# Attention outputs brought to head order by DMA transposes of scaled f16 parts, with a reordered prologue

## Chip, cores and metric

The kernel runs on one core of one Trainium2 chip. The metric is the device time of one execution in microseconds (us); less is better. All weights and the hidden states start in device memory and the result is written back there.

## What is computed

One transformer layer on `h` of 2 x 1024 tokens x 256 channels, 16 heads of width 128, one shared key and value head:

```python
q = rmsnorm(rope(h @ Wq_c @ Wq_up)) * q_norm_w           # 16 heads x 128
k = rmsnorm(rope(h @ Wk)) * k_norm_w;  v = h @ Wv
ck = rmsnorm(h.reshape(b, 64, 16*256) @ W_comp)          # one compressed key per block of 16 tokens
c_out  = softmax([q @ ck.T * s  (earlier blocks only), sink]) @ ck
sw_out = softmax([50*tanh(q @ k.T * s / 50)  (last 64 tokens), sink]) @ v
ao = c_out + sw_out
x = layernorm(h + (ao grouped by 4 heads @ Wg).reshape(...) @ Wo)
y = layernorm(x + x @ ternary(ffn_weight).T + bias)
```

The kernel folds `Wg` and `Wo` into one matrix per head, `Weff` (128 x 256), and multiplies the compressed values with it once (`CW`), so that the compressed half of the attention goes straight from probabilities to the 256 output channels.

## The kernel before

**Tiles and steps.** The 2048 tokens are 16 tiles of 128. One loop (`all_steps`) is written out in full, once for each engine, for steps i = -1 to 17. In step i the engines work on four tiles at once: the queries of tile i+1 (`front`), the attention of tile i (`mid`), the output projection and first norm of tile i-1 (`proj`), and the feed forward part and second norm of tile i-2 (`ffn`). A tile looks at `n = groups(i)` = i mod 8 + 1 groups of 8 compressed keys, so the compressed scores, their exponentials, the transposes of their probabilities and the products with `CW` grow with n.

**Order.** There is no planner. Each engine (TensorE = PE, VectorE = DVE, ScalarE = ACT, GpSimd = POOL, SyncE = SP) has its instructions in a fixed order, written by hand, and waits on counting semaphores. So an instruction that waits holds back all that stands behind it on its engine.

**One step on PE**: queries of the next tile (line 443, banks 0 to 3), transposes of `x1` (519), 12 window score matmuls (546) with the feed forward matmuls (526) between them, compressed scores (560), 36 matmuls of the projection of the tile before (600, heads 0 to 11, `EARLY`), the product of the probabilities with `V` for the first 64 queries (621, `values(0)`), the remaining 12 projection matmuls, the products with `CW` (579), `values(1)`, the transposes of the compressed probabilities (639, `probs_T`), and 16 transposes of the attention output `ao` into PSUM (648, `output_T`). Only then the next step's queries.

**Three products for one.** Where f32 accuracy is wanted, an operand is split in a high part and the rest (`PARTS`: high x high, low x high, high x low). The projection takes `ao` and `Weff` in f32r parts: ACT writes the high part of the transposed `ao` from PSUM (`narrow`, line 672), DVE the rest (`output_rest`, line 1027).

**DVE in a step**: sums of squares of the queries (945), the second norm's sum `z` (953, it waits for `g_out`, the result of the tile before, since `z` has one buffer), rope of half the queries (963, 964), the maximum of the compressed scores (974), the rest of rope, the norm (993), `divide(0)` (1009 to 1020), `query_rest` (1035), the first norm's sum (1045), `divide(1)`, then `output_rest` twice.

**ACT in a step**: two squares of queries (731), the copy of the transposed `x1`, four tanh (745), two exp (749), 16 exponentials of compressed scores (758), the f16 part of the queries (line 672 by way of `narrow`, which writes `room_K`), the copy of the transposed probabilities, and the two high parts of `aoT`.

**POOL in a step**: a power for the query norm (1112), two masks (1106), the normalisation of the compressed probabilities (1120), a power (1126), `x1` (1130), `x1` plus bias (1134), and the result (1137, `g_out`).

**SP in a step**: four DMA transposes of the queries (350), f16, 128 partitions x 1024 elements each, which PE's window scores wait for (`s_qt`), and the output (365).

**Prologue.** Loads, transposes of `h`, keys and values, compressed keys, then `xcT` (the latent queries), the transposes of `Wg`, the key norm and rope, the ternary weights, `Weff` (484 and 721, rest on DVE 934), `CW` (506), which goes through device memory (`cw_rows`) to be laid out by block. In step -1 ACT writes all eight high parts of `Weff` (`output_weights`) and then the two f16 parts of tile 0's queries.

## Time and profile before

| | |
|---|---|
| median of 3 runs | 455.08 us (454.64 to 455.99) |
| profiled execution, its own time | 455.08 us |
| its span, first to last instruction | 453.1 us, so 2.0 us lie around it |
| PE busy | 407.7 us (90%) |
| DVE busy | 351.8 us (78%) |
| ACT busy | 277.0 us (61%) |
| POOL busy | 227.7 us (50%) |
| granted TensorE clock, mean | 0.97 of full speed |

Matmuls overlap on PE, so the duration of one (some 280 ns) is longer than the distance to the next; the chain of work gives the length of a whole group. A wait is listed in brackets with what ended it. The first window scores start at 77.4 us; from there to 406.9 us the loop runs 15 times, and the last stretch to 453.1 us has no queries of a next tile.

### The profile page before, as it was taken

What the parts mean: (1) busy time and instruction counts of PE and PEld (TensorE: products, weight loads), DVE (VectorE), ACT (ScalarE), POOL (GpSimd) and SP (SyncE); (2) the same over time, 40 slices, a digit from 0 to 9 for tenths busy, and PEclk for the clock granted to TensorE, in tenths of its full rate; (3) what the DMA queues carried; (4) which work ended last, traced back from release to release, by engine and by line L of the source; (5) the groups of instructions that cost most, each with busy time, mean ns of one, the idle gap of its engine ahead of it and who ended that gap; (6) DMA issues with size and microseconds to landing.
All of it is one profiled execution on the core that took longest, in us unless ns stands there. A gap on an engine that the chain in (4) does not pass through costs nothing.

```text
span 453.1 us, 9004 instructions
## 1 busy us (share of the span) xinstructions
PE 407.7 (90%) x3361; PEld 350.7 (77%) x3363; DVE 351.8 (78%) x668; ACT 277.0 (61%) x802; POOL 227.7 (50%) x151
## 2 busy tenths in 40 slices
PE   6997888599898999999999999898989999998991
PEld 5996777479696878787879797787788888887880
DVE  3557897788898988889788878888798898972422
ACT  3556527857667675858484848584859595847200
POOL 2743120606456565656564636565546565654505
PEclk9999699889999999999999999999899999999997
DMA  8990007292242406040605060406050604060000
GB/s 257 259 341 9 1 0 210 94 255 53 44 59 48 93 14 94 14 93 13 95 13 93 13 92 16 93 13 95 12 94 13 94 14 93 14 94 13 0 13 23
DMA packets 80651, 33.43 MB, mean 74 GB/s; under 512 B 68960, under 2 KB 79200, under 8 KB 80352
## 3 DMA queue, kind: packets, MB, share of 16 engines
q1 hardware_dynamic: 79792, 32.53, 33.4%
q8 instruction: 27, 0.44, 0.4%
q10 hardware_dynamic: 816, 0.33, 0.3%
q14 instruction: 16, 0.13, 0.1%
HBM read 11.87 MB, written 4.19 MB: 35 GB/s over the span
## 4 chain that ended last, share of the span: by engine, by line
PE 59%; DVE 16%; issue 9%; ACT 9%; POOL 3%; DMA 2%; SPq 1%; POOLq 0%; ACTq 0%; DVEq 0%
PE PS L600 12%; PE PS L546 9%; PE PS L621 9%; PE PS L443 5%; ACT room_h L758 5%; PE PS L560 4%; DVE room_wg L1020 4%; PE PS L579 4%; PE PS L648 3%; PE PS L526 3%; PE PS L405 3%; DVE room_K L1035 2%; DVE aoT L1027 2%; PE PS L484 2%; PE PS L422 2%
## 5 line engine op out<-in xcount | busy, mean ns | idle before, releaser
L600 PE MATMUL PS<-Weff,aoT 128*128 128x256 f32 x768 | 97.1, 282 | 0.0
L600 PEld LDWEIGHTS PS<-Weff,aoT 128*128 128x128 f32 x768 | 91.6, 188 | 0.1
L1112 POOL TENSOR_TENSOR ny<-nx,nu 128x16 f32<-128x16 f32 x16 | 46.7, 2920 | 89.0 <-DVE nx L947 89.0
L1106 POOL TENSOR_TENSOR room_wg<-room_comp,keep 128x1024 f32<-128x1024 f32 x32 | 75.9, 2394 | 6.2 <-ACT room_comp L749 6.2
L621 PE MATMUL PS<-V,room_wg 128*128 128x129 f32 x512 | 67.8, 283 | 6.9 <-POOL room_wg L1106 2.5
L621 PEld LDWEIGHTS PS<-V,room_wg 128*128 128x128 f32 x512 | 63.4, 196 | 11.1 <-ACT room_h L758 4.0
L758 ACT ACTIVATE room_h<-PS,room_K 128x8 f32<-128x8 f32 (+7 forms) x256 | 70.4, 363 | 1.8 <-DVE room_K L974 1.7
L758 ACT ACTIVATION_READ_ACCUMULATOR room_h<-PS,room_K 128x1 f32 x256 | 62.0, 248 | 0.0
L672 ACT ACTIVATE room_wo<-PS 128x128 f32<-128x128 f32 (+7 forms) x16 | 10.4, 651 | 75.1 <-PE PS L639 75.1
L1027 DVE TENSOR_TENSOR aoT<-PS,aoT 128x1024 fp32r<-128x1024 f32 x32 | 38.9, 1224 | 16.8 <-ACT aoT L672 16.5
L546 PE MATMUL PS<-room_h,kT 128*128 128x512 f16 x192 | 46.5, 379 | 2.5 <-DVE aoT L1027 1.3
L648 PE MATMUL PS<-ident,room_wg 128*128 128x128 f32 x256 | 35.2, 282 | 14.6 <-DVE room_wg L1020 14.2
L1126 POOL TENSOR_TENSOR ny<-nx,nu 128x2 f32<-128x2 f32 (+1 forms) x17 | 11.6, 682 | 70.0 <-DVE nx L1054 70.0
L745 ACT ACTIVATE room_comp<-PS 128x512 f32<-128x512 f32 x64 | 36.7, 604 | 15.8 <-PE PS L546 15.6
L672 ACT ACTIVATE aoT<-PS 128x1024 fp32r<-128x1024 f32 x32 | 32.8, 1024 | 21.1 <-PE PS L648 20.9
L648 PEld LDWEIGHTS PS<-ident,room_wg 128*128 128x128 f32 x256 | 28.9, 144 | 19.2 <-DVE room_wg L1020 18.4
L1020 DVE TENSOR_TENSOR room_wg<-PS,r 128x768 f32<-128x768 f32 x64 | 41.3, 686 | 1.1
L945 DVE TENSOR_REDUCE ssq<-room_wg 128x8 f32<-128x1024 f32 x32 | 37.7, 1211 | 3.0 <-ACT room_wg L731 2.8
L443 PE MATMUL PS<-wqup_p,xcT 128*128 128x512 f32 x128 | 36.2, 420 | 2.6 <-DVE xcT L874 1.5
L1035 DVE TENSOR_TENSOR room_K<-PS,room_K 128x1024 f16<-128x1024 f32 x32 | 37.7, 1219 | 0.5
L993 DVE TENSOR_TENSOR PS<-PS,ny 128x1024 f32<-128x1024 f32 x32 | 37.7, 1223 | 0.0
L1120 POOL TENSOR_TENSOR room_h<-room_h,room_K 128x112 f32<-128x112 f32 (+7 forms) x16 | 22.2, 1386 | 26.5 <-DVE room_K L1013 26.5
(151 smaller groups left out, 744.6 us busy)
## 6 DMA issues: line engine op xcount, KB each, us to landing
H<-in_L_attn_h SPq DMA_DIRECT2D x4, 512.0 KB, 6.3
room_wg<-in_L_attn_Wg SPq DMA_DIRECT2D x1, 2048.0 KB, 15.3
cw_rows<-room_wgT SPq DMA_DIRECT2D x1, 2048.0 KB, 6.8
CW<-cw_rows SPq DMA_DIRECT2D x1, 2048.0 KB, 8.1
out<-room_wo SPq DMA_DIRECT2D x16, 128.0 KB, 1.7
CW<-in_L_attn_Wq_up SPq DMA_DIRECT2D x2, 512.0 KB, 12.3
room_wo<-in_L_attn_Wo SPq DMA_DIRECT2D x1, 1024.0 KB, 17.7
room_h<-room_K SPq DMA_TRANSPOSE x64, 3.3
```

The costliest lines, as they stand in the source:

```text
L443: last = nc.tensor.matmul(qbank(hf)[:, (n % 2) * 512:(n % 2 + 1) * 512], xcT[:, t * P:(t + 1) * P], wqup_p[:, w, n * 512:(n + 1) * 512], s ...
L546: last = nc.tensor.matmul(bank(b), kT[:, kp, at + c * WIN:at + c * WIN + P], qT[:, qp, 8 * hf:8 * hf + 8, c * WIN:(c + 1) * WIN], start=n ...
L600: last = nc.tensor.matmul(o, aoT[:, ap, hd // 2, hd % 2, :, :].rearrange("p c q -> p (c q)"), Weff[:, wp, hd, :], start=mid and hd == n == ...
L621: last = nc.tensor.matmul(pv, Pm[:, c, 2 * pr:2 * pr + 2, :], V[:, 2 * i + c, :], start=True, stop=True)
L648: last = nc.tensor.transpose(bank((2, 4)[c], 2)[:, pr * P:(pr + 1) * P], ao[:, c, pr, :], ident[:, :])
L672: nc.scalar.activation(dst, src, ACT.Copy).then_inc(s, 1)
L758: last = nc.scalar.activation(Ec[:, 0:n, hd], bank(4 + hd // 8)[:, (hd % 8) * n:(hd % 8 + 1) * n], ACT.Exp, bias=mn[:, hd:hd + 1], accum_o ...
L1020: last = V_.tensor_tensor(o, pv, r, ALU.mult)
L1027: V_.tensor_tensor(aoT[:, 1, :, :, c, :], bank((2, 4)[c], 2).rearrange("p (a r q) -> p a r q", r=2, q=WIN), aoT[:, 0, :, :, c, :].bitcast( ...
L1035: V_.tensor_tensor(qp[:, 1, heads, :], by_head(hf), qp[:, 0, heads, :], ALU.subtract).then_inc(d_ql, 1)
L1106: G.tensor_tensor(Pm[:, c, :, :], E[:, c, :, :], keep[:, :, :], ALU.mult).then_inc(g_mask, 1)
L1112: G.tensor_tensor(ny[:, 0:HEADS], nx[:, 0:HEADS], nu[:, 0:HEADS], ALU.pow).then_inc(g_rs, 1)
```

## The change

- The 16 PE transposes of `ao`, ACT's and DVE's splits of them from PSUM, and the semaphores p_at and d_al go. Instead ACT writes `ao` in f16 from SBUF to SBUF (`output_high`, one for each half c of the tile), POOL writes the rest in f16 (`output_low`; the first behind line 1120, the second behind line 1134 and ahead of line 1137), and SP issues four DMA transposes for each tile (`outputs`), each of 64 partitions x 2048 elements of f16.
- `Weff`, `ckTv` and `aoT` are f16. So that f16 holds them, the values and `Weff` are scaled by powers of two, worked out in the prologue from sums of squares (`total`, `norms`, `unit`); DVE takes the scale out again in the first norm's sum.
- The projection is 32 matmuls with the high part (`project_high`), then, behind `values(0)`, 16 with the low part (`project_low`).
- The transposed probabilities use banks 2 and 3, not 0 and 1.
- On ACT the first square of the next-but-one tile's queries stands between the copy of the transposed probabilities and `output_high(1)`.
- Prologue: other order of loads (`Wq_up` behind `Wg`), of PE's groups (queries of tile 0 and key transposes ahead of the transposes of `Wg`), key rope before the key norm, the ternary weights on POOL, eight sums of squares on ACT, tile 0's f16 queries written between the high parts of `Weff`, some fifteen small chained instructions on DVE for the scales, the rests of `Weff` (`weights_rest`) spread over more places in step -1, a room of its own for `staged`, and the read of `CW` issued ahead of tile 1's query transposes.

```diff
@@ sync: new, behind queries(i + 1) in each step
+            def outputs(i):
+                wait(sp, p_o, i)
+                for n, ready in ((0, a_at), (1, g_al)):
+                    sp.wait_ge(ready, 2 * i + 2)
+                    for r in range(2):
+                        sp.dma_start(aoT[:, n, r, :, :].rearrange("p a (c q) -> p (a c) q", q=WIN),
+                                     ao16[r * WIN:(r + 1) * WIN, n, :, :, :].rearrange("p a c d -> p (a c d)"),
+                                     transpose=True).then_inc(s_ah if n == 0 else s_al, 16)
@@ tensor: step
-                    wait(pe, *((d_al, 2 * t - 3) if hf else (a_ct, t - 1)))
+                    wait(pe, d_ql, 2 * t + hf - 1)
+                    if hf:
+                        wait(pe, a_ct, t - 1)
...
-                    pe.wait_ge(a_at, 2 * t + 2)
-                    pe.wait_ge(d_al, 2 * t + 2)
...
+                    pe.wait_ge(s_ah, 32 * t + 32)
+                def project_high():
+                    for hd in range(HEADS):
+                        for wp in range(2):
+                            last = nc.tensor.matmul(o, aoT[:, 0, hd % 2, hd // 2, :], Weff[:, wp, hd, :],
+                                                    start=mid and hd == wp == 0, stop=False)
+                def project_low():
+                    pe.wait_ge(s_al, 32 * t + 32)
+                    for hd in range(HEADS):
+                        last = nc.tensor.matmul(o, aoT[:, 1, hd % 2, hd // 2, :], Weff[:, 0, hd, :],
+                                                start=False, stop=not mid and hd == HEADS - 1)
...
-                def output_T(c):
-                    pe.wait_ge(d_ao, 2 * i + c + 1)
-                    for pr in range(PAIRS):
-                        last = nc.tensor.transpose(bank((2, 4)[c], 2)[:, pr * P:(pr + 1) * P], ao[:, c, pr, :], ident[:, :])
-                    last.then_inc(p_at, 1)
@@ scalar: step
-                    def output_T(c):
-                        act.wait_ge(p_at, 2 * i + c + 1)
-                        narrow(aoT[:, 0, :, :, c, :], bank((2, 4)[c], 2).rearrange("p (a r q) -> p a r q", r=2, q=WIN), a_at)
+                    def output_high(c):
+                        act.wait_ge(d_ao, 2 * i + c + 1)
+                        wait(act, s_ah, 32 * i)
+                        narrow(ao16[:, 0, :, c, :], ao[:, c, :, :], a_at)
+                    output_high(0)
                     act.wait_ge(p_ct, i + 1)
...
+                    if i + 2 < NT:
+                        square(i + 2, 0)
+                    output_high(1)
@@ vector: step
-                    wait(dve, p_at, 2 * i + c - 1)
+                    wait(dve, g_al, 2 * i + c - 1)
...
-                def output_rest(c):
-                    dve.wait_ge(a_at, 2 * i + c + 1)
-                    V_.tensor_tensor(aoT[:, 1, :, :, c, :], bank((2, 4)[c], 2).rearrange("p (a r q) -> p a r q", r=2, q=WIN),
-                                     aoT[:, 0, :, :, c, :].bitcast(f32), ALU.subtract).then_inc(d_al, 1)
@@ gpsimd: step
+                def output_low(c):
+                    pool.wait_ge(a_at, 2 * i + c + 1)
+                    wait(pool, s_al, 32 * i)
+                    G.tensor_tensor(ao16[:, 1, :, c, :], ao[:, c, :, :], ao16[:, 0, :, c, :], ALU.subtract).then_inc(g_al, 1)
@@ scalar: prologue
+                    nc.scalar.mul(Weff[:, 0, 2 * g:2 * g + 2, :], two(G_WE + g), w_unit).then_inc(s_wh, 1)
+                    if g in (4, 5):
+                        act.wait_ge(s_ps, G_CKT + 1)
+                        query_high(0, g - 4)
@@ vector: prologue
+            dve.wait_ge(s_ps, G_SC + 1)
+            V_.tensor_copy(total[:, :], gbank(G_SC)[:, 0:8]).then_inc(s_evd, 1)
+...
+            link(V_.reciprocal(unit[:, 0:2], unit[:, 2:4]))
+            V_.tensor_tensor(o_inv[:, :], v_inv, w_inv, ALU.mult).then_inc(s_unit, 1)
@@ gpsimd: prologue
+            G.tensor_scalar(fw_a[:, :, :], fw_s[:, :, :], fthr[:, 0:1], fscale[:, 0:1], ALU.is_gt, ALU.mult)
+            pool.wait_ge(s_fth, 2)
+            G.tensor_scalar(fw_b[:, :, :], fw_s[:, :, :], fthn[:, 0:1], fscale[:, 0:1], ALU.is_lt, ALU.mult).then_inc(s_fth, 1)
+            pool.wait_ge(s_fth, 3)
+            G.tensor_tensor(wfT[:, :, :], fw_a[:, :, :], fw_b[:, :, :], ALU.subtract).then_inc(s_fw, 1)
```

## Rows read from the trace of the kernel before

**Rows 1.** Stages: length, busy us of PE, PEld, DVE, ACT, POOL, PE clock, DMA share
```profile
77.00:98.60 21.60, 16.02 (x124) 12.54 (x125) 16.59 (x30) 14.18 (x46) 7.94 (x4) 0.84 0.60 176
...
162.00:183.70 21.70, 20.79 (x187) 17.93 (x185) 19.38 (x37) 15.17 (x47) 13.01 (x8) 1.00 0.36 57
...
229.20:253.40 24.20, 23.15 (x195) 19.67 (x194) 20.14 (x37) 15.91 (x47) 13.83 (x8) 1.00 0.28 50
...
297.50:320.50 23.00, 21.12 (x180) 17.98 (x179) 20.29 (x38) 15.03 (x47) 12.47 (x8) 0.93 0.35 59
...
406.90:453.10 46.20, 33.44 (x259) 28.73 (x260) 14.51 (x34) 13.71 (x45) 17.24 (x14) 0.93 0.04 12
```

**Rows 2.** Chain of work: start, length, what; last row from a later step
```profile
164.35 1.29 PE PS L546 x6
...
167.11 4.18 PE PS L600 x36
...
172.64 0.73 PE PS L621 x4
...
180.60 1.09 PE PS L648 x8
181.69 1.83 PE PS L443 x8
...
245.99 1.79 PE PS L621 x16
```

**Rows 3.** DVE in the step from 162.1 us, idle time before in brackets
```profile
164.69 0.42 DVE L953 TENSOR_TENSOR room_wo<-PS,room_h 128x256 f32<-128x256 f32 x1
...
175.21 2.36 DVE L1035 TENSOR_TENSOR room_K<-PS,room_K 128x1024 f16<-128x1024 f32 x2
...
179.25 1.29 DVE L1020 TENSOR_TENSOR room_wg<-PS,r 128x768 f32<-128x768 f32 x2
180.86 1.22 DVE L1027 TENSOR_TENSOR aoT<-PS,aoT 128x1024 fp32r<-128x1024 f32 x1 [0.32 <-ACT aoT L672]
```

**Rows 4.** ACT in that step: first exponential, then the f16 parts of the queries
```profile
168.07 0.32 ACT L758 ACTIVATE room_h<-PS,room_K 128x40 f32<-128x40 f32 x1
...
172.38 2.02 ACT L672 ACTIVATE room_K<-PS 128x1024 f16<-128x1024 f32 x2
```

**Rows 5.** POOL in that step: the result
```profile
181.75 1.22 POOL L1137 TENSOR_SCALAR room_wo<-room_wo,mv,ny 128x256 f32<-128x256 f32 x1
```

**Rows 6.** POOL in the prologue
```profile
41.24 1.17 POOL L1086 TENSOR_TENSOR room_comp<-room_K,rope_s 128x256 f32<-128x256 f32 x1 [10.23 <-DVE room_K L876]
...
43.52 0.73 POOL L1086 TENSOR_TENSOR room_comp<-room_K,rope_s 128x256 f32<-128x256 f32 x1
...
47.73 1.90 POOL L1092 TENSOR_TENSOR keep<-CW,e 128x1024 f32<-128x1024 f32 x1 [2.81 <-ACT e1w L709]
```

**Rows 7.** Groups by line: shapes, xcount, busy us, mean ns, idle time before
```profile
L1106 POOL TENSOR_TENSOR room_wg<-room_comp,keep 128x1024 f32<-128x1024 f32 x32 | 75.9, 2394 | 6.2 <-ACT room_comp L749 6.2
...
L579 PE MATMUL PS<-CW,room_wo 128*128 128x256 f32 (+1 forms) x144 | 33.7, 379 | 0.0
```

**Rows 8.** DMA transposes of line 350: ns of SP to issue, us to landing
```profile
L350 SPq DMA_TRANSPOSE room_h<-room_K x64: 1231/1327/2367, 69.7 to 402.3; - x64
...
DMA to landing us min/median/max: 3.2/3.3/5.1
```

**Rows 9.** Chain of work from the weights to the first window scores
```profile
56.47 2.36 DVE ssq L945 x2
...
68.63 1.94 ACT room_K L672 x2
...
73.93 3.34 DMA room_h<-room_K
77.40 2.77 PE PS L546 x12
```

**Rows 10.** Last tile: transposes of its attention output on PE
```profile
427.67 2.27 PE L648 MATMUL PS<-ident,room_wg 128*128 128x128 f32 x16
```

More of the change, by code:

```diff
@@ L382, in _ @@
             pe.wait_ge(s_id, 2)
-            for n in range(12):
+            for n in range(14):
                 nc.tensor.transpose(bank(7)[:, 0:P], ident[:, :], ident[:, :])
@@ L445, in queries @@
                     last.then_inc(p_q, 1)
-            for g in range(G_WG - 8, G_WG):
-                if g % 8 < 4:
-                    copied(pe, g)
-            pe.wait_ge(s_up, 1)
-            pe.wait_ge(s_lo, 4)
-            queries(0)
+            pe.wait_ge(s_up, 2)
+            pe.wait_ge(s_lo, 1)
+            for g in (9, 10, 11, G_CK):
+                copied(pe, g)
+            queries(0)
+            pe.wait_ge(s_kn, 1)
+            for g in range(4):
+                b = begin(G_KT + g)
+                for t in range(4):
+                    last = nc.tensor.transpose(b[:, t * P:(t + 1) * P], K[:, 4 * g + t, :], ident[:, :])
+                end(last)
+            pe.wait_ge(s_kn, 2)
+            b = begin(G_CKT)
+            end(nc.tensor.transpose(b[:, 0:P], K[:, NT, :], ident[:, :]))
             pe.wait_ge(s_wg, 16)
@@ L461, in _ @@
                 end(last)
-            pe.wait_ge(s_kn, 1)
-            for g in range(4):
-                b = begin(G_KT + g)
-                for t in range(4):
-                    last = nc.tensor.transpose(b[:, t * P:(t + 1) * P], K[:, 4 * g + t, :], ident[:, :])
-                end(last)
-            b = begin(G_CKT)
-            end(nc.tensor.transpose(b[:, 0:P], K[:, NT, :], ident[:, :]))
+            pe.wait_ge(s_tot, 8)
+            b = begin(G_SC)
+            end(nc.tensor.matmul(b[:, 0:8], ones[:, :], total[:, :], start=True, stop=True))
             pe.wait_ge(s_fs, 1)
@@ L693, in _, with squares, latent @@
             nc.scalar.activation(sqk, K[:, 0:NT, :], ACT.Square).then_inc(s_sq, 1)
-            if by_scalar[G_CK]:
-                evac(G_CK, K[:, NT, :], gbank(G_CK)[:, 0:D])
-            for g in range(4):
+            def squares(n, data):
+                wait(act, s_tot, n)
+                nc.scalar.activation(junk.rearrange("p (a d) -> p a d", d=data.shape[2]), data, ACT.Square,
+                                     accum_out=total[:, n:n + 1]).then_inc(s_tot, 1)
+            def latent(g):
                 act.wait_ge(s_ps, G_XC + g + 1)
@@ L723, in step @@
             def step(i, front, mid, proj, ffn):
-                if front:
-                    for hf in range(2):
-                        act.wait_ge(p_q, 2 * i + 3 + hf)
-                        if i == -1:
-                            act.wait_ge(s_ps, G_WG + 8)
-                        wait(act, d_red, 2 * i + 2)
-                        wait(act, p_pv, 2 * i)
-                        nc.scalar.activation(sq[:, 8 * hf:8 * hf + 8, :],
-                                             qbank(hf).rearrange("p (a d) -> p a d", d=D),
-                                             ACT.Square).then_inc(a_sq, 1)
+                if front and i < 1:
+                    square(i + 1, 0)
@@ L978, in step @@
                 if first:
[L979 removed]
+                    weights_rest(1)
                 if front:
@@ L987, in step @@
                         last.then_inc(d_add, 1)
+                if first:
+                    weights_rest(2)
                 if front:
```

304 lines of the change are left out of this document (174 added, 130 removed).

## The prediction

> **What bounds the kernel now.** I read the stages first [rows 1]. From 77.4 to 406.9 us the loop makes 15 rounds, 329.5 us in all. The step from 162 us (n = 5) is typical: 21.7 us, PE busy 20.8, DVE 19.4, ACT 15.2, POOL 13.0. PE leads, but DVE is only 1.4 us behind it, so I followed the chain of work next. In this step it leaves PE after the product with `V` (172.64), runs through DVE's `divide(0)`, `query_rest`, the first norm's sum and `divide(1)` (ends at 180.54), and comes back with the second batch of transposes of `ao` at 180.60, for which PE had stood idle about 0.9 us; then queries, then window scores at 183.7 [rows 2, 3]. So two things hold the step: PE's own queue, and the way over DVE and back. At n = 8 the step is 24.2 us with PE busy 23.2: there it is PE's queue alone [rows 1]. Two stages ran at less than full clock (0.84 in the first, 0.93 from 297.5) [rows 1]. Then I read each engine's own list in the one step, to see who gets slack and who gets work.
>
> **PE, what goes.** 16 transposes: two batches of 1.09 = 2.2 us at most (the first partly overlaps what is ahead), and the 0.9 us idle between them [rows 2]: about 2.9 us at n = 5, 2.0 where PE didn't wait. The projection stays 48 matmuls of 256 columns. Now 36 take 4.18, 116 ns each [rows 2]. An f16 one of 512 columns takes 1.29 / 6 = 215 ns [rows 2], so 256 columns take 107 if columns set the pace and 116 if nothing is gained; I take 110, a gain of 0.3 us a step, bounds 0 to 0.4. By its own queue PE would need 21.7 - 2.9 - 0.3 = 18.5 us at n = 5. It won't get there, because of what follows.
>
> **DVE** loses two operations of 1.22 us [rows 3]: 2.4 us off 19.4, so 17.0. The scale in the first norm's sum adds an operand that is one number for each partition: nothing, at most 0.1.
>
> **ACT** writes the same number of elements, from SBUF and not from PSUM. The nearest row is its f16 part of the queries, 2.02 / 2 = 1.01 us for 1024 elements [rows 4]; I take 1.0, bounds 0.8 to 1.2. No work is added, but the order changes: `output_high(1)` now stands behind `probs_T`'s copy and the square of the next-but-one tile, and this square waits for the first half of its queries on PE.
>
> **POOL** gets two `output_low` of 1024 elements a step. No row has this operation with f16. The masks, same size and two inputs, take 2.39 us [rows 7]; one operation of that size with broadcast inputs took 1.90 [rows 6]; and the rope product took 1.17 us for 256 elements while DVE was also at work, 0.73 after DVE had stopped [rows 6], that is 4.7 us for 1024 at the worst. I take the mask's 2.4, since it runs in the same loop beside the same DVE, bounds 1.9 to 4.7. POOL goes from 13.0 to 17.8 us: not full. But the second one stands **ahead of the result (1137)**, and DVE's `z` (953) waits for the result of the tile before, having one buffer. Before, the result ended at 182.97 and the next `z` came some 3.3 us later [rows 3, 5], so nobody saw this wait. 2.4 us more, plus the later start behind `output_high(1)`, eat it up.
>
> On this the Trainium skill (GPSIMD Engine Reference, specifications) says that POOL shares its SBUF interfaces with DVE and that they contend with DVE instructions that have two SBUF inputs. The two rope rows agree. In the loop DVE's large operations read PSUM, so by that rule the slow price doesn't apply.
>
> **The new round (R).** It closes over four engines. At n = 5, from rows: `z` to the first exponential 168.07 - 164.69 = 3.4, less about 0.4 in which DVE waited for the scores = 3.0; 16 exponentials 172.38 - 168.07 = 4.3 [rows 3, 4]; the last quarter of the product with `V` 0.7 [rows 2]; 16 low matmuls at 110 ns 1.8; products with `CW` of the tile before, 4 groups at 33.7 / 72 = 0.47, less the slow stages = 1.8 [rows 7]; `values(1)` 1.8 [rows 2]; 5 transposes of probabilities (0.5) and half the queries (0.9) with the way to ACT, 1.7 [rows 2]; the square 1.0; `output_high(1)` 1.0 [rows 4]; `output_low(1)` 2.4; the result 1.2 and two hand-overs 0.1 [rows 5]. Sum **20.8 us**. Per further group it grows by about 0.9 (exponentials and maximum 0.3, `CW` 0.45, transposes 0.1 and so on): 21.7, 22.6, 23.5 for n = 6, 7, 8.
>
> **The short round (S)**, for small n, goes by DVE alone: `z` 164.69 to the end of `divide(1)` 180.54 is 15.9, less the 0.4 = 15.5 [rows 3]; then `output_high(1)`, `output_low(1)` and the result, 4.7: 20.2 at n = 5, 0.13 less per group: 19.7 to 20.0 for n = 1 to 4.
>
> **DMA and SP.** SP now issues 8 transposes a step, not 4: 8 x 1.33 = 10.6 us [rows 8]. One step's DMA share of 0.28 to 0.36 [rows 1] is 6 to 8 us, mostly four transposes, 1.4 to 1.6 us each. The new ones have the same number of elements in half the partitions and twice the length; no row shows this shape. From 1.4 (same bytes) to 2.8 us (half the partitions, half the speed), I take 1.4. Then all DMA work is about 12 of 20 us. The high pair goes out when `output_high(1)` is done and lands 1.3 + 3.3 = 4.6 us after; PE's projection stands some 6 us behind (window scores 2.6, feed forward 1.0, compressed scores 1.4, and the wait for the queries). The low pair follows 2.7 us later and PE takes it behind 32 matmuls (3.5) and `values(0)` (2.0). So both are hidden, with some 1 to 2 us to spare. The queries' own four stand ahead of them in SP's order and don't wait; the output DMA behind them comes later but `res` has time.
>
> **The loop.** Round by round: the first two have no result and no `z` to wait for, 19.2 (low clock) and 18.0 against 21.2 and 20.4; n = 3, 4: 19.9 and 20.0; n = 5 to 8: 20.8, 21.7, 22.6, 23.5; second sequence: 20.6 (n = 1, but `CW` of an n = 8 tile), 19.8, 19.9, 20.0, 20.8, 21.7, 21.4. Sum 309.9 against 329.5: **-19.6 us**. A stage at lower clock cost about 1.5 us once in this loop [rows 1]; I add 1.2 for one of the same kind, as PE now has more gaps.
>
> **Tail.** The 16 transposes, 2.27 us on PE [rows 10], go, 0.3 us of projection too. The high pair lands about 4.6 us after ACT, while PE does the feed forward and `CW` products (4.6 us), so nearly no new wait: 46.2 [rows 1] becomes 43.8, **-2.4**.
>
> **Prologue.** Up to the queries of tile 0 (about 38.8 us) PE and the loads set the pace; `Wq_up` now comes behind `Wg`, and its low part on POOL (4.5 us) ends about when PE wants it: 0, bounds 0 to +2. From there DVE was the bound. It loses the ternary weights to POOL (2 us) and does the rope work earlier, where it was idle, but gets some fifteen chained steps of 0.2 us for the scales: I put the first sum of squares at 54.8 and not 56.5 [rows 9]. In step -1 before, ACT wrote the f16 queries only after the eighth high part of `Weff` (68.63), and the four issues and the last landing then led to 77.40 [rows 9]. Now they stand behind the fifth and sixth; DVE's order is then 15.0 us from its start to the end of the last `query_rest`, 69.8, and 3.3 us to landing: 73.2. PE has by then the last `CW` weights and queries, 73.9 or so. I take **-3.3**, bounds +1 (late `Wq_up`, ACT's eight sums of squares of 1.2 us each ahead of the weights) to -5.
>
> **Sum.** 453.1 - 19.6 + 1.2 - 2.4 - 3.3 = 429.0, and 2.0 us around the span: **431.0 us**. The profiled execution is the median itself (455.08), so nothing is to be shifted.
>
> **Rivals.**
> 1. *The new transposes are slow, 2.8 us each.* Then the high pair lands after PE wants it. Each round becomes about 0.6 us longer, the tail 4: 444. Against it: same bytes, same packets by my guess; for it: half the partitions. 10 in 100.
> 2. *They are so slow that the DMA queue is the bound.* It decides from (20.5 - 4 x 1.4) / 4 = 3.7 us each; at 4.5 us each a round is 5.6 + 18 = 23.6 at least, plus their latency in round after round: 16 x 2.5 + 6 more than the forecast, 477. **Slower.** 7 in 100.
> 3. *POOL at 3.8 us for `output_low`* (the price beside a DVE that reads SBUF). Every round R and S grows by 1.4, or more where both count: 452 to 458, about 455, no change. 5 in 100. At 3.0 us it would be 440, in my range.
> 4. *POOL's f16 operation is faster*, 1.3 us: rounds fall to PE's queue and DVE's, 19.2 or so: 420. 12 in 100.
> 5. *No gain in the prologue or a loss there by the late loads*, loop as forecast: 436. In the range.
> 6. *The change doesn't do what it says*, another wait takes DVE's and PE's gain in full: 450 to 458. 4 in 100.
>
> **Chances.** Forecast with its neighbours (422 to 442) 62 in 100. The range 418 to 446 takes in rivals 1 and 4 and leaves rivals 2, 3 and 6 out. Differences of 0.3% (1.4 us) are about what a measurement here can tell from no change. Rivals 3 and 6 end on both sides of no change. Faster 0.87, within 0.3% 0.05, slower 0.08.
>
> **What would show it.** Right: window scores start near 74; line 648's work is gone; at n = 5 a step of 20 to 21 us; DVE's `z` shows an idle time ended by POOL's result; PE busy below 19 us a step with waits ahead of window scores or the last quarter of `values(0)`. Wrong: PE waits for a transposed `ao` ahead of the projection (rival 1 or 2); `output_low` above 3 us (3) or under 1.5 (4); window scores start at 77 or later (5).

## The result, and the profile after

The changed kernel takes **442.2 us** (median of 4 runs, 440.2 to 444.7) where the kernel before, on the same chip, takes 454.9: a ratio of 0.972, with a 95% interval of 0.968 to 0.977. It is faster, inside the range of 418 to 446, 11 us above the forecast of 431.0 and just outside its neighbourhood (422 to 442). Medians here are over all runs of a kernel; ratios and their intervals leave out single runs more than 1.5% above the fastest of the same kernel. The profiled execution took 440.81 us with a span of 439.0, so 1.8 us lie around it. Its parts beside the forecast (window scores start, fifteen rounds, tail):

| | before | forecast | after |
|---|---|---|---|
| first window scores | 77.4 | 74.1 | 78.5 |
| first two rounds | 41.4 | 37.2 | 42.1 |
| other thirteen rounds | 288.1 | 272.7 and 1.2 for the clock | 273.8 |
| tail | 46.2 | 43.8 | 44.6 |
| span | 453.1 | 429.0 | 439.0 |

Before and after, the stretches run from the start of one tile's window scores to the next one's. The other thirteen rounds sum to what was forecast, to 0.1 us, but that is in part luck. One by one, the seven with n of 5 and more were 0.2 to 1.5 us shorter than forecast (4.4 together), and the six with smaller n were 0.1 to 2.2 us longer (5.5 together). Of the miss of 10.0 us, 4.9 lie in the first two rounds, 4.4 in the prologue and 0.8 in the tail.

The stages of the kernel after (columns as in [rows 1]: length, busy us of PE, PEld, DVE, ACT and POOL, granted clock, DMA share, GB/s): the first two rounds, the step at n = 5, the first round of the second sequence, the tail.

```profile
78.50:99.20 20.70, 14.98 (x109) 12.26 (x109) 14.59 (x27) 13.83 (x47) 10.08 (x5) 0.67 0.78 244
99.20:120.60 21.40, 17.50 (x158) 13.51 (x158) 16.50 (x32) 14.79 (x47) 14.52 (x9) 0.92 0.64 100
161.30:181.30 20.00, 18.73 (x171) 15.30 (x169) 16.70 (x35) 14.88 (x47) 17.07 (x11) 1.00 0.74 113
...
247.70:270.50 22.80, 21.10 (x176) 17.16 (x174) 16.58 (x34) 14.08 (x47) 15.63 (x10) 0.93 0.62 100
394.40:439.00 44.60, 30.87 (x244) 24.74 (x244) 10.25 (x30) 13.75 (x45) 24.53 (x18) 0.93 0.36 60
```

At n = 5 PE has 2.1 us less to do than in [rows 1], DVE 2.7 less, POOL 4.1 more, and the DMA share went from 0.36 to 0.74. No engine is busy for the whole step, so waits have a part in closing it. Which ones, the list of waits says, first of the kernel before (PE), then of after (PE, then DVE); columns: who waited for whom, us in total, times, longest.

```profile
PE PS L648 <- DVE room_wg L1020: 14.2, 13, 1.9
```

```profile
PE PS L628 <- DMA aoT<-ao: 26.1, 16, 2.6
PE PS L548 <- POOL room_wo L1219: 10.8, 9, 3.7
...
DVE room_wo L1022 <- POOL room_wo L1228: 18.6, 14, 4.6
```

Before, PE waited 1.1 us a step for DVE ahead of its transposes of `ao`. That wait is gone with the transposes, and a longer one is there instead: 1.6 us a step ahead of the projection's high halves (line 628), for the DMA. And `z` (1022) waits for the result (1228) in 14 steps, as the forecast's round R has it. Both are to be seen in one step, in the chain of work of after (start, length, what):

```profile
161.74 2.09 POOL ao L1184
163.84 1.22 POOL room_wo L1228
...
165.18 0.44 DVE room_wo L1022
...
168.02 2.92 ACT room_h L815 x21
...
172.61 0.71 PE PS L657 x4
173.32 1.75 PE PS L636 x16
175.06 1.73 PE PS L608 x8
176.80 1.79 PE PS L657 x16
178.58 0.55 PE PS L675 x5
179.13 0.94 PE PS L466 x4
...
181.02 1.05 ACT ao L697
...
182.14 1.24 SPq L368
...
183.43 5.09 DMA aoT<-ao
...
188.65 3.65 PE PS L628 x32
```

From `output_low(1)` (1184) over the result, `z`, the exponentials (815) and PE's list to `output_high(1)` (697) is round R, term by term. The chain then leaves it at 182.1: not to POOL, but over SP's issue and the landing to PE. So a step has **two ends**. POOL's list shows that the other one is alive at the same time; the result ends at 185.49, and the next `z` starts 20.4 us after the one in the chain:

```profile
182.14 2.14 POOL L1184 TENSOR_TENSOR ao<-room_wg,ao 128x1024 f16<-128x1024 f32 x1 [0.34 <-ACT ao L697]
184.25 1.24 POOL L1228 TENSOR_SCALAR room_wo<-room_wo,mv,ny 128x256 f32<-128x256 f32 x1
```

The groups whose price the forecast had to guess, of after (SP's issue in ns min/median/max, landing in us; the group of 1184 as in [rows 7]):

```profile
L1184 POOL TENSOR_TENSOR ao<-room_wg,ao 128x1024 f16<-128x1024 f32 x32 | 68.3, 2135 | 28.7 <-ACT ao L697 28.6
...
L368 SPq DMA_TRANSPOSE aoT<-ao x64: 1241/1833/3057, 100.2 to 421.4; - x64
...
DMA to landing us min/median/max: 3.6/4.4/6.4
```

POOL's low half is 2.14 us (2.4 assumed) and ACT's high half 1.05 (1.0, line 697 in the chain). The transposes are dearer than assumed. Their queue, of before and of after (packets, MB, share of 16 engines):

```profile
q1 hardware_dynamic: 79792, 32.53, 33.4%
```

```profile
q1 hardware_dynamic: 147376, 49.31, 62.4%
```

0.624 x 439.0 - 0.334 x 453.1 = 122.6 us more in the queue for 64 more transposes: 1.9 us each, not 1.4.

### The profile page after: what moved, and what is told of

It reads as the page before. It is cut to its first block, busy times and chain, and to the rows that moved or that the text cites. A ratio compares the mean times of both kernels' runs of the same rounds, so it can differ in the third digit from the quotient of the medians.

```text
span 439.0 us, 8659 instructions
## 1 busy us (share of the span) xinstructions
PE 373.6 (85%) x3109; PEld 307.7 (70%) x3111; DVE 321.5 (73%) x647; ACT 287.8 (66%) x818; POOL 302.7 (69%) x190
## 3 DMA queue, kind: packets, MB, share of 16 engines
q1 hardware_dynamic: 147376, 49.31, 62.4%
## 4 chain that ended last, share of the span: by engine, by line
PE 34%; ACT 16%; DVE 13%; POOL 12%; DMA 11%; issue 10%; SPq 2%; POOLq 0%; ACTq 0%; DVEq 0%
ACT room_h L815 9%; PE PS L657 8%; DMA aoT<-ao 7%; PE PS L628 6%; POOL ao L1184 5%; PE PS L608 5%; ACT ao L697 3%; PE PS L636 3%; PE PS L466 3%; DMA room_h<-room_K 3%; PE PS L426 3%; PE PS L575 2%; SPq L368 2%; POOL room_wo L1228 2%; DVE room_K L1100 2%
## 5 line engine op out<-in xcount | busy, mean ns | idle before, releaser
L1184 POOL TENSOR_TENSOR ao<-room_wg,ao 128x1024 f16<-128x1024 f32 x32 | 68.3, 2135 | 28.7 <-ACT ao L697 28.6
L628 PE MATMUL PS<-Weff,aoT 128*128 128x256 f16 x512 | 61.4, 281 | 26.1 <-DMA aoT<-ao 26.1
L1194 POOL TENSOR_TENSOR room_wg<-room_comp,keep 128x1024 f32<-128x1024 f32 x32 | 74.7, 2358 | 1.1 <-ACT room_comp L806 1.1
L628 PEld LDWEIGHTS PS<-Weff,aoT 128*128 128x128 f16 x512 | 50.4, 100 | 34.6 <-issue 26.5
L1200 POOL TENSOR_TENSOR ny<-nx,nu 128x16 f32<-128x16 f32 x16 | 46.8, 2925 | 18.1 <-DVE nx L1016 18.1
L1014 DVE TENSOR_REDUCE ssq<-room_wg 128x8 f32<-128x1024 f32 x30 | 36.5, 1220 | 21.8 <-ACT room_wg L766 21.5
L697 ACT ACTIVATE ao<-room_wg 128x1024 f16<-128x1024 f32 x32 | 33.7, 1055 | 27.5 <-DVE room_wg L1091 27.3
L466 PE MATMUL PS<-wqup_p,xcT 128*128 128x512 f32 x128 | 37.7, 433 | 3.5 <-POOL wqup_p L1158 2.9
L766 ACT ACTIVATE room_wg<-PS 128x1024 f32<-128x1024 f32 x30 | 30.6, 1024 | 5.6 <-PE PS L466 5.4
L697 ACT ACTIVATE room_K<-PS 128x1024 f16<-128x1024 f32 x32 | 32.6, 1119 | 2.2 <-DVE PS L1064 2.2
L608 PE MATMUL PS<-CW,room_wo 128*128 128x256 f32 (+1 forms) x144 | 33.8, 379 | 0.0
```

The lines of the kernel that those rows point to most:

```text
L466: last = nc.tensor.matmul(qbank(hf)[:, (n % 2) * 512:(n % 2 + 1) * 512], xcT[:, t * P:(t + 1) * P], wqup_p[:, w, n * 512:(n + 1) * 512], s ...
L608: last = nc.tensor.matmul(o, PcT[0:rows, g, :], CW[0:rows, TPB * (t // TPB) + g, :], start=start and g == 0, stop=not start and g == end)
L628: last = nc.tensor.matmul(o, aoT[:, 0, hd % 2, hd // 2, :], Weff[:, wp, hd, :], start=mid and hd == wp == 0, stop=False)
L697: nc.scalar.activation(dst, src, ACT.Copy).then_inc(s, 1)
L1184: G.tensor_tensor(ao16[:, 1, :, c, :], ao[:, c, :, :], ao16[:, 0, :, c, :], ALU.subtract).then_inc(g_al, 1)
L1194: G.tensor_tensor(Pm[:, c, :, :], E[:, c, :, :], keep[:, :, :], ALU.mult).then_inc(g_mask, 1)
```

## Experiments

**Two ends, taken away one at a time.** The first edit puts the result ahead of `output_low(1)` on POOL, so that `z` no longer waits behind it:

```diff
-                if mid:
-                    output_low(1)
                 if ffn:
                     pool.wait_ge(s_out, 16 * i - 16)
                     G.tensor_scalar(res[:, :], z[:, :], ...).then_inc(g_out, 1)
+                if mid:
+                    output_low(1)
```

> The changed kernel with one edit: on GpSimd the result of the tile (g_out) is written ahead of the second subtraction of the low part, not behind it. Theory A (the round closes over the low part, the result and z): z's idle time ended by the result, 18.6 us in all in the changed kernel, goes to under 3; the rounds with n = 5 to 8 shrink by 0.2 to 0.7 us each, about 3 us less in all, 438 to 440. Theory B (the output transposes' landing sets the rounds): no change within 0.5 us, and TensorE's wait for the transposed outputs stays near 1.7 us a step. The pair of low transposes starts 1.2 us later and may give part of it back.

442.4 us, ratio 0.968 (0.960 to 0.977). The first condition did what was meant, and the time stayed within its interval of the changed kernel's 0.972:

```profile
PE PS L628 <- DMA aoT<-ao: 26.9, 15, 2.5
...
DVE room_wo L1022 <- PE PS L555: 11.1, 3, 5.5
```

`z` waits no more for POOL, but PE waits for the DMA as long as before. So neither expectation held in full. The rounds of n = 7 and 8 did shrink as the first one had it (21.6 and 22.2 us for 22.1 and 22.9), but the median didn't follow.

The second edit makes the transposes the size of the queries' own, 128 partitions x 1024 elements, one for each window. It leaves out the order of heads and tokens that the projection needs, so the output is another one: it prices the shape and isn't a version to use.

```diff
-                    for r in range(2):
-                        sp.dma_start(aoT[:, n, r, :, :].rearrange("p a (c q) -> p (a c) q", q=WIN),
-                                     ao16[r * WIN:(r + 1) * WIN, n, :, :, :].rearrange("p a c d -> p (a c d)"),
+                    for c in range(2):
+                        sp.dma_start(aoT[:, n, c, :, :], ao16[:, n, c, :, :].rearrange("p a d -> p (a d)"),
                                      transpose=True).then_inc(s_ah if n == 0 else s_al, 16)
...
```

> The changed kernel, with the four output transposes of a tile taken as 128 partitions x 1024 elements (one for each half c) in place of 64 partitions x 2048, issued at the same times. The order of heads and tokens in aoT is then not the reference's, so the values are not; times and counts of instructions are unchanged. It prices the shape. Theory B (half the partitions cost more): a transpose takes 1.4 us of all 16 DMA engines and not 1.9, so the DMA share of the span falls from 0.62 to about 0.48, the landing from 4.4 to 3.3 us, and the time by 4 to 6 us. Theory A (the round closes over GpSimd and z): the landing improves as well, but the rounds with n = 5 to 8 keep 20.1, 21.3, 22.1, 22.9 us; the gain is 1 to 2 us, from the first rounds and the tail.

437.0 us, ratio 0.960 (0.953 to 0.967). The issue and the landing, and what PE and DVE wait for:

```profile
L368 SPq DMA_TRANSPOSE aoT<-ao x64: 1232/1338/2196, 97.0 to 411.7; - x64
...
DMA to landing us min/median/max: 3.2/3.3/5.4
...
PE PS L627 <- DMA aoT<-ao: 11.9, 12, 2.1
...
DVE room_wo L1021 <- POOL room_wo L1227: 18.6, 14, 4.6
```

So the shape costs 0.5 us in the issue and 1.1 in the landing, for the same 49.31 MB. The queue's share fell from 62.4% to 58.3% of a span of 431.8 us, which makes 1.6 us of the 16 engines for each of these transposes, where 1.4 was expected. PE's wait for the DMA halves, `z`'s for POOL remains. Each theory had a half of it: the time fell by 5.2 us, and yet the rounds of n = 6, 7 and 8 kept their length, as the table below shows. Both edits together:

> Both the output transposes over whole partitions (heads come out in another order, so the output is another one; the work is as much) and the result ahead of the second low half on POOL. Theory that a round has two ends of about equal length, the next z behind POOL's low half and result, and the landing of the output transposes: each edit alone left the other end (442.4 and 437.0), both together take about 1 us more from each of 13 undisturbed rounds, loop 296 to 302 us where it was 309 with the transposes alone, time 427 to 431. Rival that z is not an end at all: time as with the whole partitions alone, 437 within 2.

432.6 us, ratio **0.948** (0.945 to 0.951). The result's place is worth 1.2 points behind the better transposes, where alone its 0.4 were no more than the spread. That the two together give 0.8 points more than the sum of both alone is what two ends would do, but it isn't clear of the four intervals. The rounds of the profiled execution sum to 307.5 us, against 309.1 with the transposes alone and 315.9 after; I had expected 296 to 302: the sign of the joint effect held, its size didn't. (In this profile one round more than after, the one at n = 6, fell to a clock of 0.92.)

The single rounds show the two ends better than the medians do (us from one tile's window scores to the next one's, in each profiled execution; a star marks a round below full clock):

| | n = 5, 6, 7, 8 | second sequence, n = 2, 3, 4 |
|---|---|---|
| changed kernel | 20.1, 21.3, 22.1, 22.9 | 20.3, 21.0, 20.9 |
| result first | 19.9, 21.5, 21.6, 22.2 | 22.0*, 20.9, 20.5 |
| whole blocks | 19.6, 21.2, 22.1, 22.9 | 19.9, 19.6, 19.8 |
| both | 19.4, 22.8*, 21.1, 22.2 | 19.2, 19.4, 20.0 |

At n = 7 and 8 only the result's place moves the round: round R closes it. The other profiles below that have this round unchanged and at full clock there (three of the prologue, and the first of the clock) have 22.1 and 22.9 too. The short rounds move mainly with the better transposes: there it is the landing.

**The same, with the right order of heads.** PE can cover the landing with work of its own that needs no transposed `ao`, the products with `CW` of the tile before:

```diff
-                    if not mid:
-                        project_blocks(True, range(groups(t)))
+                    project_blocks(True, range(groups(t)))
                     pe.wait_ge(s_ah, 32 * t + 32)
...
-                    project_low()
-                    project_blocks(False, range(groups(t))).then_inc(p_o, 1)
+                    project_low().then_inc(p_o, 1)
```

> The products of the compressed values (one to eight matmuls of 0.22 us) go ahead of the wait for the output transposes instead of behind the low halves: the same matmuls, the same sum. Theory that the landing of the transposes ends each round on PE and that this new wait took back a part of what was won: PE's idle time ahead of the high halves falls from 26 us to 12 to 16, the loop from 315.9 to 304 to 309 where nothing else binds, time 432 to 437. Rival that the other end, z behind POOL's low half and result, takes over at once: time 438 to 441, and only with the result ahead of the low half does the rest come.

443.5 us, ratio 0.970 (0.966 to 0.975): no gain that can be told, although most of the wait went.

```profile
PE PS L548 <- POOL room_wo L1217: 17.1, 14, 3.7
PE PS L627 <- DMA aoT<-ao: 7.0, 5, 3.1
...
DVE room_wo L1020 <- POOL room_wo L1226: 14.0, 13, 4.7
```

19 us of the wait for the DMA are gone, 6 us come back as a wait for `x1` from POOL (1217) and some 8 us as short waits for DVE. The fifteen rounds sum to 313.8 us for 315.9. What the rounds gained was lost elsewhere in this profile: the tail took 47.5 us for 44.6, at a clock of 0.82 for 0.93 (the two versions that build on this one have 47.7 and 0.82 as well), and the window scores started 1.8 us later. `z` still waits for the result in 13 steps, which looks like the other end. With the result first as well:

> Blocks ahead of the heads on PE and the result ahead of the second low half on POOL. Theory of two ends: 3 to 6 us less than with the blocks alone, 428 to 433. Rival that z is no end once the blocks are moved (DVE gets y 1.7 us earlier, which moves all that POOL does behind it): same as with the blocks alone within 2 us.

440.9 us, ratio 0.967 (0.963 to 0.970): 2.6 us less than the blocks alone, under the 3 to 6 that the two ends gave and within the spread. `z`'s wait for POOL is gone from the list, and still no round from n = 3 on changed by more than 0.3 us; they sum to 313.2 us for 313.8. At n = 7 and 8 both have 21.2 and 21.8. So with the blocks first `z`'s wait closes no round any more, as the rival had it. A reason that fits, not tested by itself: the edit takes the products with `CW`, a term of round R, out of that round too. Then with the high part of each window sent as soon as ACT has it:

```diff
-                for n, ready in ((0, a_at), (1, g_al)):
-                    sp.wait_ge(ready, 2 * i + 2)
-                    for r in range(2):
+                for c in range(2):
+                    sp.wait_ge(a_at, 2 * i + c + 1)
+                    for r in range(2):
+                        sp.dma_start(aoT[:, 0, r, :, c * WIN:(c + 1) * WIN],
+                                     aoh[r * WIN:(r + 1) * WIN, c, :, :].rearrange("p a d -> p (a d)"),
+                                     transpose=True).then_inc(s_ah, 16)
+                sp.wait_ge(g_al, 2 * i + 2)
+                for r in range(2):
...
```

> As the one before, and the high part of each window of the outputs is sent as soon as ACT has it: six transposes in a round instead of four, the four high ones half as long. Theory that the high part of the first window lands in the shade of the second and the wait ends 1 us earlier where it still stands: 1 to 3 us less than the one before, 427 to 431. Rival that SP's issues (1.2 us each, ten in a round where there were eight) and the queues' load push the low part and the queries' landing back: 2 to 6 us more than the one before.

433.8 us, ratio **0.951** (0.947 to 0.955): 7 us less than without it, where one theory had 1 to 3 us less and the other 2 to 6 more. The transposes of the high part land in 2.7 us, and round 1 (columns as above) and PE's longest waits are

```profile
98.20:116.90 18.70, 16.77 (x158) 12.76 (x158) 16.65 (x32) 14.91 (x47) 14.67 (x9) 1.00 0.72 111
...
PE PS L553 <- POOL room_wo L1222: 17.2, 14, 3.7
```

with no wait of PE's matmuls for `aoT` in the list. The fifteen rounds sum to 306.7 us. What fell are mostly rounds with few blocks to cover the landing (n = 2 from 21.2 to 18.7, and in the second sequence n = 2, 3, 4 to 19.2, 19.4, 19.7); n = 7 and 8 stay at 21.2 and 21.8. This version computes the same as the changed kernel and is 1.9% below it by the medians (433.8 against 442.2, measured against two sets of runs of the kernel before). PE's longest wait in it is now for POOL's `x1`, 1.2 us a step; whether that is what closes the steps wasn't tested.

**A low half on DVE.** The second window's low part goes from POOL to DVE, behind `divide(1)`:

```diff
-                    output_low(1)
...
+                    dve.wait_ge(a_at, 2 * i + 2)
...
+                    V_.tensor_tensor(ao16[:, 1, :, 1, :], ao[:, 1, :, :], ao16[:, 0, :, 1, :], ALU.subtract).then_inc(d_al, 1)
```

> The low half of the outputs' second window goes from POOL (2.1 us, ahead of the result) to DVE, right behind the division. Theory that POOL's low halves set the rounds: the transposes start about 1.2 us earlier and z no longer waits for POOL, so 0.7 to 1.2 us less in each round, loop 300 to 306 us for 316, time 428 to 434. Rival that DVE is the tighter engine: it waits for ACT's high half (1.05 us) and then works for 0.6 to 1.2 us ahead of the next reduction, so each round keeps its length or grows by up to 1 us: 442 to 452.

449.1 us, ratio 0.983 (0.979 to 0.987): slower than the changed kernel, as the rival had it. DVE does the operation in 1.23 us, POOL in 2.13, but DVE stands idle ahead of it (the list puts this down to issue; in the step at n = 5 it ended at 181.47, just behind ACT's high half at 181.39):

```profile
DVE ao L1137 <- issue: 21.6, 15, 2.1
...
PE PS L633 <- DMA aoT<-ao: 27.2, 15, 2.6
```

1.4 us a step of standing in front of everything else on DVE, and PE's wait isn't shorter. Its rounds of n = 4 to 8, at full clock, are 0.0 to 0.2 us longer than those of the changed kernel, some 2 us over the loop; in its profile six rounds were below full clock (0.82 to 0.93), where the changed kernel had three. By the rounds that is the larger part of its 7 us; whether the edit brings the lower clock about isn't shown.

**The clock.** In one run PE does transposes of no use in the two gaps of round 0 (30 and 14 of them), where the clock had been 0.67:

> The changed kernel with 30 transposes of the identity ahead of the first product with V in the first round, and 14 ahead of its second, where TensorE waits 3.7 and 2.0 us. Theory C (these waits drop the granted clock to half, and the products with V then take 3.8 us for 1.8): the clock of the first round goes from 0.67 to above 0.9, the first round from 20.7 to 18.5 to 19.5 us, and the time falls by 1.5 to 3 us. If the clock falls all the same, no change within 0.5 us.

445.9 us, ratio 0.977 (0.971 to 0.984).

```profile
80.60:98.70 18.10, 15.72 (x153) 12.88 (x152) 15.33 (x28) 14.82 (x48) 10.10 (x5) 1.00 0.89 279
```

Round 0 has its full clock and takes 18.1 us instead of 20.7, so these gaps cost 2.6 us. The time isn't better for it: rounds 1, 2 and 9 had 0.92 or 0.93, and the tail took 48.7 us at 0.83 where it had taken 44.6 at 0.93. In another run eight such transposes stand in every step ahead of the wait for `aoT`:

> Eight idle transposes of the identity (about 0.14 us each, 1.1 us together, their result is overwritten) on PE in each of rounds 1 to 15, between the block scores and the wait for the output transposes, which was 1.6 us long on average. Nothing else changes, so the high halves start when the DMA lands, as before. Theory that PE's standing still at this wait is what the clock falls on (stretches of 3.4 to 4 us at half clock began within 2 us of such a wait in each profile so far, 1.7 us lost each): two to four of these stretches go, granted clock 0.965 to 0.975 instead of 0.947 to 0.965, time 436 to 440. Rival that the clock falls whatever PE does there: clock as now, time 442 to 444.

444.5 us, ratio 0.975 (0.970 to 0.980): no gain. PE's wait fell to 13.7 us and the clock of its runs (0.959 to 0.972) is somewhat above that of the changed kernel (0.947 to 0.965), but rounds 1, 6 and 10 still fell to 0.92 or 0.93. That the clock falls on this wait alone isn't borne out. What speaks for it all the same: the three versions with the blocks first, where the wait is nearly gone, had the full clock in all rounds from 2 to 14 of their profiles (though 0.82 in the tail). Which idle time it is that costs the clock stays open.

**The prologue.** First `Wq_up` ahead of the rope table and `Wg` in the loads:

```diff
+            for r in range(2):
+                sp.dma_start(wqup_s[r * QC:(r + 1) * QC, :], wqup).then_inc(s_wq, 16)
             sp.dma_start(rope_s[:, :, :], rope_t).then_inc(s_tab, 16)
             sp.dma_start(wg_s[:, :, :], ...).then_inc(s_wg, 16)
-            for r in range(2):
-                sp.dma_start(wqup_s[r * QC:(r + 1) * QC, :], wqup).then_inc(s_wq, 16)
```

> The changed kernel with Wq_up loaded ahead of the rope table and Wg, as before the change. Theory: its late landing (33.8 us) put GpSimd's low part of it at 35.9 to 40.4 and the first queries at 40.5 instead of 38.8, and made a small DVE product beside it take 2.8 us. If this sets the start of the loop, window scores start 1.5 to 2.5 us earlier, at 76 to 77. If the sums of squares on ScalarE and the scale's chain set it, they start at 78 to 78.5 as now.

442.1 us, ratio 0.967 (0.958 to 0.977), first window scores at 79.4, no earlier. ACT had the weights 3.5 us earlier (30.37 for 33.86), but that doesn't clear the late load. POOL's low part of these weights (1158) now met another small operation of DVE with two SBUF inputs, 16 elements each, which held DVE for 4.6 us:

```profile
32.34 4.62 POOL L1158 TENSOR_TENSOR wqup_p<-CW,wqup_p 128x2048 fp32r<-128x2048 f32 x1 [2.22 <-ACT wqup_p L734]
```

```profile
32.40 4.59 DVE L873 TENSOR_TENSOR nu<-nx,ny 128x16 f32<-128x16 f32 x1
```

DVE's `xcT` came late by it, and PE's first queries began at 39.9, only 0.6 us earlier. The other profiles show the load itself at work. With the order of loads of the change, ACT takes the weights at 31.5 to 35.5 us,

```profile
33.86 1.92 ACT L734 ACTIVATE wqup_p<-CW 128x2048 fp32r<-128x2048 f32 x1 [3.28 <-DMA CW<-in_L_attn_Wq_up]
```

and in all twelve profiles PE's first queries begin 6.6 us behind that: two operations of ACT's and POOL's on the weights lie between. So the late load does set the first queries, and most of the spread in the start of the window scores is the spread of this landing. Then the units as constants:

```diff
-                nc.scalar.activation(junk..., data, ACT.Square, accum_out=total[:, n:n + 1]).then_inc(s_tot, 1)
...
+            for n, x in enumerate((32.0, 128.0, 1.0 / 32, 1.0 / 128)):
+                V_.memset(unit[:, n:n + 1], x)
...
```

The squares and the chain of small operations that made the units are gone with it.

> The units are constants of a power of two (32, 128 and their inverses) instead of being worked out from sums of squares: the eight squares on ACT (1.05 us each with 0.19 us behind them, 9.9 us together), the wait of PE and POOL for them and the chain of ten small operations on DVE (54.0 to 56.4 us) are gone; the scaling itself stays. Theory that the squares stand on the way to the first queries: the chain of the changed kernel runs through two pairs of them at 45.2 and 46.9 us, between the key transposes, for 2.2 us, and DVE's chain holds its first reduction at 57.2 us for up to 0.8 us, so the first window scores go from 78.5 to 75.5 to 76.5 us and the time from 442.2 to about 439.5. Rival that they are covered by POOL's low half of the query weights and by DVE's own list: the first window scores move by less than 0.5 us and the time stays 442.

442.8 us, ratio 0.970 (0.967 to 0.974): by the time, the rival. The window scores started at 76.8, and DVE's first sum of squares, at 55.46, now follows ACT directly. But the ten profiles with the changed kernel's own prologue start at 76.0 to 80.8 us (78.5 after, 79.1, 76.6, 78.5 in the first three runs above), so the start alone can't show 1.7 us. Counted from ACT's operation on the weights it can: 43.8 us to the window scores, where the changed kernel took 44.6, and eight of the ten 44.4 to 45.6 (two took 46.7 and 47.2, unexplained). So by this one profile the units cost some 0.8 us, not 2 to 3. Last, the weights' low parts 5, 6 and 7 ahead of the queries' low halves:

> The last three low parts of the output weights (0.65 us each) ahead of both low halves of the first queries on DVE (1.13 us each) instead of between and behind them. Theory that PE's matmuls of the compressed values behind the last low part set the start: they begin 2.2 us earlier and the first window scores move from 78.5 to 76.3 to 76.8 us, where the landing of the first queries takes over (low half ends 73.2, 3.3 us to land); time 440. Rival that something behind them, the mask or the exps of round 0, sets the second round: start earlier, first round longer by as much, time 442.

445.7 us, ratio 0.976 (0.972 to 0.980), first window scores at 78.3. Its profiled execution, at 450.1, was the longest of its six, with a clock of 0.941, so only its prologue is read. DVE reached the last low part earlier and stood waiting for PE and ACT to make the weights themselves: PE's last eight products for them began at 68.64, ACT's high part at 70.64, and DVE's low part at 71.36, where it had been 71.90. From DVE's first sum of squares to the window scores it took 21.0 us, where all others took 21.3 or 21.4: the move, meant to bring 2.2 us, gains 0.3.

## Why the prediction was right or wrong

**Round R, right.** At n = 5 the rows above give: `z` to the first exponential 2.8 (3.0 assumed), exponentials 4.5 (4.3), the last quarter 0.7, low matmuls 1.75, `CW` 1.7, `values(1)` 1.8, transposes and half the queries 1.5 (1.7), the square with its hand-over 0.9, `output_high(1)` 1.05, `output_low(1)` 2.1 (2.4), the result 1.2. That is 20.0, and 20.4 from one `z` to the next with the hand-overs; the round took 20.0, where the sum said 20.8. At n = 6, 7, 8 the rounds are 21.3, 22.1 and 22.9 for 21.7, 22.6 and 23.5. Also right: DVE lost its two operations, PE's queue came down to 18.7 us, its f16 projection runs at 3.65 / 32 = 114 ns (110 assumed). The short round S was right where the landing is out of the way: with the whole blocks the rounds of n = 2 to 4 in the second sequence took 19.9, 19.6 and 19.8, for 19.8, 19.9 and 20.0. In the changed kernel they took 0.5 to 1.1 us more than forecast. So the sum of the thirteen rounds met the forecast because R was put 0.4 to 0.8 us too high and the landing behind S was left out: with the stage at lower clock, the errors cancel, by luck.

**"Both are hidden, with 1 to 2 us to spare": failed.** That is the step on the output transposes. It had two sizes wrong. The landing of the high pair is 1.24 + 5.09 = 6.3 us behind ACT in the step shown, not 4.6, and each transpose is 1.9 us of DMA, not 1.4 (in the whole shape it would be 1.6). Rival 1 had the direction (half the partitions, slower) and too high a price. The trace had no row for this shape, and I took the lower bound by the bytes. PE waits 1.6 us a step for it, which the forecast named as the sign that the step is wrong. It cost nothing at n = 7 and 8, because round R ended those at the same time, and 2.9 us in the short rounds of the second sequence: with the better shape alone the time falls by 1.3 points (some 6 us), not by 26 us.

**The first two rounds, failed by 4.9 us.** They were taken as PE's and DVE's short rounds, since nothing waits for a result there. But the two things that R hides elsewhere stand bare here. Round 0: PE stands 3.7 us for POOL's mask and then works at half clock until about 98.5 us; the stage had 0.84 before and has 0.67 now, worth 2.6 us by the run with the busy PE. Round 1: 2.3 us of waiting for the first transposed outputs, and behind them the clock is at half for a while, so that the projection's 32 matmuls take 4.96 us:

```profile
86.72 3.81 PE L657 MATMUL PS<-V,room_wg 128*128 128x129 f32 x16 [3.74 <-POOL room_wg L1194]
...
106.07 4.96 PE L628 MATMUL PS<-Weff,aoT 128*128 128x256 f16 x32 [2.28 <-DMA aoT<-ao]
```

The same 32 matmuls take 3.65 us at full clock. The run with blocks and result first, at full clock, still needed 21.2 us for this round, with a wait of 2.8; the run with the early high part has no wait and 18.7. So the landing is the larger part of the 3.4 us by which this round missed, and without it the round comes within 0.7 us of the 18.0 forecast.

**The prologue, failed by 4.4 us: rival 5.** Two halves. The first sum of squares came at 57.2 us and not at 54.8, and from there to the window scores it took 21.3 us, not 19.3:

```profile
40.47 3.69 PE PS L466 x8
...
57.16 2.36 DVE ssq L1014 x2
...
71.90 0.67 DVE Weff L1003
72.70 4.09 PE PS L533 x36
76.80 1.84 PE PS L466 x8
78.64 2.62 PE PS L575 x12
```

In the second half I let the chain end with the queries' landing (73.2) and put PE's `CW` matmuls beside it. They stand behind the last low part of the weights, which DVE makes after its last `query_rest`: 4.1 and 1.8 us, the last terms of the chain, were left out of the sum. Moving that part up didn't help because PE and ACT have the weights no sooner. In the first half the queries began 1.7 us later than the 38.8 assumed, and that is the late load: the forecast took 0 for it, with +2 as its bound. ACT had the weights at 33.86, and the queries stand 6.6 us behind. The other 0.7 us lie between the queries and the first sum of squares (16.7 us, for 16.0 forecast); the run without squares and scales is 0.8 us shorter from the weights on.

**The tail** came out 0.8 us above 43.8: PE waited 0.75 us for the last `aoT`, where I had "nearly no new wait".

**The clock allowance** of 1.2 us was short of what one stage took (0.93, 22.8 us where 20.6 were forecast, and 20.5 to 21.7 where the same round had the full clock in other profiles) and missed rounds 0 and 1. Over the runs the changed kernel's clock was 0.947 to 0.965, where the kernel before has 0.963 to 0.979 in its eleven runs beside the run with constant units. By the rounds that fell, the lower clock takes part of the gain back.

## What to carry to other kernels

When work moves from an engine to the DMA queues, price the transfer by a row of its own shape, and where there is none, take the wait for its landing as open and not as hidden. Where two waits close a step at about the same time, a cure alone can look worthless by the median (the result first: 0.968, for 0.972), so compare the single rounds too, and try cures in pairs before you drop one (0.948 together). And when an edit moves a piece of work, look at what the moved piece collides with in its new place, before you acquit the cause that it was meant to test. Then look at the rounds that lack the usual bound, the first ones above all: what the others hide is bare there.

## What the hardware showed that I hadn't expected

- A DMA transpose of 64 partitions x 2048 elements took 1.9 us of the 16 engines, 1.83 us to issue and 4.4 to land (medians); of 128 x 1024, as many bytes, 1.6 us of them, 1.34 to issue and 3.3 to land; of 64 x 1024, 1.27 and 2.7.
- A product of two SBUF inputs, 128 elements, took 2.78 us on DVE while POOL worked on the low half of the query weights (35.9 to 40.4 us). The same product before, with POOL idle, took 0.29:

```profile
37.78 2.78 DVE L940 TENSOR_TENSOR room_comp<-room_K 128x128 f32<-128x128 f32 x1
```

```profile
L866 DVE TENSOR_TENSOR room_comp<-room_K x1: 291/291/291, 32.0 to 32.0; 128x128 f32<-128x128 f32 x1
```

  The Trainium skill (GPSIMD Engine Reference, specifications) says that POOL and DVE instructions with two SBUF inputs contend. The trace agrees, and here the price was on DVE's side: the small operation ended at 40.56 us, just behind POOL's at 40.41. In the run with the query weights first the same product ran behind POOL's operation and took 0.29 us, and the 16-element operation that stood beside it instead took 4.59 and ended at 36.99, just behind POOL's at 36.96; other 16-element ones of the same line took 0.18.
- In the loop a power on POOL took 0.70 us for two elements of each partition (1215) and 2.92 for 16 (1200), and 0.57 for one. A single one in the prologue (1161, one element) took 2.55 us in each of the thirteen profiles that have it. A DVE operation of 2.28 us with two SBUF inputs (943) starts 0.16 us ahead of it each time, and the power ends 0.4 us behind that one's end: it looks like the same contention with the price on POOL's side, but no run parts the two.
